# Mamba fronts, tails and column copies divided anew, and the expert bias moved to the front, in a two-layer decoder kernel on one core

## The reference

```python
def mamba(h, inproj, convw, convb, xproj, dtw, dtb, Alog, Dp, outproj):
    xz = jnp.einsum('bld,ed->ble', h, inproj)
    xc, z = jnp.split(xz, 2, axis=-1)
    xc = jax.nn.silu(causal_conv(xc, convw, convb))          # four taps
    xdbl = jnp.einsum('ble,fe->blf', xc, xproj)
    dt = jax.nn.softplus(jnp.einsum('blr,er->ble', xdbl[..., :R], dtw) + dtb)
    ...
    y = ssm_scan(dt, Bm, Cm, xc, A) + xc * Dp    # h = exp(dt A) h + dt x B; y = sum over 16 states of h C
    y = y * jax.nn.silu(z)
    return jnp.einsum('ble,de->bld', y, outproj)
...
for e in range(E):
    gate_e = jnp.sum(jnp.where(top_i == e, top_w, 0.0), axis=-1)
    he = jax.nn.gelu(xf @ w1[e] + b1[e])
    out = out + gate_e[:, None] * (he @ w2[e] + b2[e])
```

## Time and profile before

| | |
|---|---|
| median of 3 runs | 2694.64 us (2692.36 to 2695.38) |
| the profiled execution | 2695.85 us, of which the trace spans 2694.0 us |
| TensorE busy | 2361.3 us (88%) |
| VectorE busy | 1870.9 us (69%) |
| GpSimd busy | 1543.2 us (57%) |
| ScalarE busy | 1339.3 us (50%) |
| layer 0 Mamba | from 3.9 to 1022.5 us, first scan at 66.15 |
| layer 1 Mamba | from 1916.3 to 2451.0 us, first scan at 1973.83 |
| experts | from 1556.1 to 1916.0 us |

### The profile page before, as it was taken

The page is one execution under the profiler, slowest core; times in us unless marked ns, Lnnn a source line. Parts: engine busy times, 40 slices in busy tenths (PEclk is TensorE's granted clock), DMA queues, the critical chain, the costliest instruction groups (busy, mean ns, idle before and its releaser), DMA issues. The chain is left out here.

```text
span 2694.0 us, 28358 instructions
## 1 busy us (share of the span) xinstructions
PE 2361.3 (88%) x8874; PEld 1077.4 (40%) x8874; DVE 1870.9 (69%) x2587; ACT 1339.3 (50%) x2213; POOL 1543.2 (57%) x1356
## 2 busy tenths in 40 slices
PE   7989899898988778888999769999889989688878
PEld 3323333333333223343433349998433333223322
DVE  2999999999999983347777241111379999994334
ACT  4556565655656443444666423332266556453333
POOL 2999999999999971150000112222179999992010
PEclk9999999999999999999999979999789999999989
DMA  4030412303031100043121059996332130300000
GB/s 179 25 125 1 143 52 84 133 10 125 1 125 52 74 0 24 19 123 63 38 39 25 6 188 329 327 329 233 105 126 79 48 125 1 125 1 22 1 9 32
DMA packets 70204, 239.03 MB, mean 89 GB/s; under 512 B 15819, under 2 KB 35799, under 8 KB 47399
## 3 DMA queue, kind: packets, MB, share of 16 engines
q1 hardware_dynamic: 58292, 183.90, 20.3%
q10 hardware_dynamic: 8018, 43.09, 4.6%
q0 software_dynamic: 3744, 10.23, 1.0%
HBM read 220.60 MB, written 16.38 MB: 88 GB/s over the span
## 5 line engine op out<-in xcount | busy, mean ns | idle before, releaser
L896 POOL TENSOR_TENSOR s_dbu<-s_dx,s_bc 128x512 f32<-128x512 f32 x768 | 968.6, 1290 | 26.4 <-DVE s_psum L564 24.8
L480 PE MATMUL s_psum<-s_hc,ident 128*128 128x512 f32 x1536 | 831.1, 634 | 151.9 <-DVE s_hc L584 131.2
L759 ACT ACTIVATE s_psum<-s_dt,s_a_neg 128x512 f32<-128x512 f32 x768 | 521.7, 688 | 576.9 <-DVE s_hc L584 576.0
L480 PEld LDWEIGHTS s_psum<-s_hc,ident 128*128 128x128 f32 x1536 | 263.8, 193 | 657.7 <-DVE s_hc L584 413.8
L584 DVE TENSOR_TENSOR s_hc<-s_psum,s_bc 128x512 f32<-128x512 f32 x624 | 419.8, 673 | 0.4 <-issue 0.4
L564 DVE TENSOR_TENSOR_SCAN s_psum<-s_psum,s_state,s_dbu 128x512 f32<-128x512 f32 x312 | 394.6, 1277 | 11.4 <-POOL s_dbu L896 6.7
L564 DVE TENSOR_TENSOR_SCAN s_psum<-s_psum,s_dbu 128x512 f32<-128x512 f32 x312 | 381.4, 1223 | 14.9 <-POOL s_dbu L896 12.5
L2015 ACT ACTIVATE s_probs<-s_banks 128x512 f32<-128x512 f32 (+3 forms) x384 | 169.6, 495 | 117.1 <-PE s_banks L1724 85.8
L2452 ACT ACTIVATE s_hidden<-s_banks,s_w 128x128 f32<-128x128 f32 x312 | 97.6, 364 | 194.3 <-PE s_banks L2244 192.5
L163 POOL TENSOR_TENSOR s_pair<-s_res 128x512 f32<-128x512 f32 x4 | 5.1, 1280 | 328.5 <-issue 327.1
L907 POOL TENSOR_TENSOR s_hc<-s_hs,s_bc 128x512 f32<-128x512 f32 x144 | 183.6, 1275 | 14.6 <-DVE s_hs L564 14.6
(11 more groups left out here) (325 smaller groups left out, 3272.6 us busy)
## 6 DMA issues: line engine op xcount, KB each, us to landing
s_bc<-fwd_rows SPq DMA_DIRECT2D x64, 1024.0 KB, 4.7
s_w<-in_moe_w SPq DMA_DIRECT2D x39, 1028.0 KB, 5.9
s_w<-in_moe_w ACTq DMA_DIRECT2D x39, 1024.0 KB, 6.8
s_bc<-m_rows SPq DMA_DIRECT2D x32, 1024.0 KB, 4.7
qk_parts<-s_parts SPq DMA_DIRECT2D x48, 128.0 KB, 1.9
s_stack_q<-qk_parts SPq DMA_DIRECT2D x96, 64.0 KB, 2.4
s_stack_k<-qk_parts SPq DMA_DIRECT2D x48, 128.0 KB, 4.4
x<-in_xT SPq DMA_DIRECT2D x4, 512.0 KB, 6.7
```

Of the source, the lines that this page charges most:

```text
L480: pe.matmul(psum[:, SCANS + block_no % 2, :], consts["ident"][:], hc[:, unit % PRODUCTS, :], start=(n == 0), stop=(n == NS - 1)).then_inc( ...
L759: act.activation(psum[:, unit % SCANS, :], dt[:, g % 2, i // NS, :], ACT.Exp, scale=a_neg[CHUNKS[g][0]][:, i:i + 1]).then_inc(decay_ready, 1)
L896: pool.tensor_tensor(dbu[:, unit % TERMS, :], dx[:, g % 2, i // NS, :], bc[:, 2 * n, :], ALU.mult)\
```

## The change

Six edits, all of order or of the engine that does a piece of work. A new small input holds the convolution's taps as columns (`fold`).

1. **Fronts of both Mambas.** The first x chunk and the x half of the weights are loaded first, the taps in two halves. VectorE scales the x half of the weights. The input products of chunk 0 are taken from the centered x and scaled behind the product, by VectorE on its way into `pad`. TensorE convolves blocks 0 and 1; VectorE convolves blocks 2 and 3 (`fold`, 8 instructions). GpSimd adds the two feature halves ahead of mean and variance, so that TensorE needs one product for each of them. dt of blocks 0 and 1 is finished first, dt of blocks 2 and 3 behind unit 2; their two last steps go to GpSimd at units 18 to 24 of chunk 0. The statistics of token chunks 2 and 3 move into chunk 0.
2. **Last columns.** VectorE's 32 `keep` copies of an even chunk become 52 copies on ScalarE, each ahead of the `decay` that overwrites the bank, with a wait in between.
3. **Tails of both Mambas.** The output products of the last chunk begin beside the last units; the last gate product, the scaling and the add to x are VectorE's, from PSUM.
4. **Expert bias.** The bias product (gate x b2) is taken at the experts' front, transposed, and added to x by VectorE in four pieces: two between `low_hot` and `source`, two behind the shares.
5. **Expert blocks.** The first input product is placed ahead of the second block's turn.
6. **Expert tail.** ScalarE multiplies row 0 by its share, VectorE joins in one instruction per tile, TensorE turns into eight banks, four pairs used once.

```diff
+            load_x(0)
             sp.dma_start(w_in[:, :, 0:EI], dram[f"{first}_in"][:, :, 0:EI]).then_inc(in_x_loaded, 16)
-            sp.dma_start(taps[:], dram[f"{first}_taps"]).then_inc(taps_loaded, 16)
+            load_x(1)
             for r, run in enumerate(runs):
                 sp.dma_start(cols[r][:], dram[f"{run[0]}_cols"]).then_inc(small_loaded, 16)
                 sp.dma_start(a_neg[r][:], dram[f"{run[0]}_alog"]).then_inc(small_loaded, 16)
+            sp.dma_start(state[:, 0:TAPS * EB], dram[f"{first}_fold"]).then_inc(small_loaded, 16)
+            sp.dma_start(taps[:, 0:KD * TAPS, :], dram[f"{first}_taps"][:, 0:KD * TAPS, :]).then_inc(taps_first_loaded, 16)
             sp.dma_start(w_x[:], dram[f"{first}_x"]).then_inc(x_loaded, 16)
...
+            def first_in_x(m):
+                if m == 0:
+                    pe.wait_ge(x_scaled, KD)
+                    pe.wait_ge(ln_centered, 1)
...
             mean(0)
+            first_in_x(0)
             mean(1)
...
+                    if g == NC - 1 and i in (58, 59):
+                        last_res(i - 58)
+                    if g == NC - 1 and i in (62, 63):
+                        for m in range(KD):
+                            last_out(m, i - 62)
+            for k in (2, 3):
+                for m in range(KD):
+                    last_out(m, k)
...
-            def keep(g, i):
-
-                unit = g * UNITS + i
-                dve.wait_ge(scanned, unit + 1)
-                at = unit % SCANS
-                if LENT[i - 1]:
-                    dve.tensor_copy(state[:, i:i + 1], psum[:, at, CH - 1:CH]).then_inc(kept, 1)
-                else:
-                    dve.tensor_copy(state[:, i - 1:i + 1].unsqueeze(2), psum[:, at - 1:at + 1, CH - 1:CH]).then_inc(kept, 1)
...
+            def keep_first_x(m):
+                dve.wait_ge(first_x, m + 1)
+                dve.wait_ge(rms_rstd_ready, 1)
+                dve.tensor_tensor(pad[:, m, TAPS - 1:TAPS - 1 + CH], first_bank(m), rms_rstd[0], ALU.mult)\
+                   .then_inc(first_kept, 1)
+            def fold(m, j):
+                tap, total_u = state[:, j * EB + m:j * EB + m + 1], u[:, 0, m, :]
+                if j == 0:
+                    dve.wait_ge(small_loaded, 32 * len(runs) + 16)
+                    dve.wait_ge(front, 1)
+                    dve.wait_ge(first_kept, m + 1)
+                    dve.tensor_scalar(total_u, pad[:, m, 0:CH], tap, None, ALU.mult).then_inc(folded, 1)
+                else:
+                    dve.wait_ge(folded, KD * (j - 1) + m - KD + 1)
+                    dve.scalar_tensor_tensor(out=total_u, in0=pad[:, m, j:j + CH], scalar=tap, in1=total_u,
+                                             op0=ALU.mult, op1=ALU.add).then_inc(folded, 1)
...
+            def last_gate():
+                e, part = EB - 1, dx[:, (NC - 1) % 2, EB - 1, :]
+                dve.wait_ge(gate_ready, NC)
+                dve.wait_ge(y_read, NC * EB)
+                dve.tensor_tensor(part, part, gate[:, e, :], ALU.mult).then_inc(last_gated, 1)
...
+            for k in range(KD):
+                scale_first_in(k)
             center(0)
             center(1)
-            scale_xn(0)
+            for m in range(KD + 1):
+                keep_first_x(m)
+            fold(2, 0)
+            keep_first_x(3)
+            fold(3, 0)
+            for j in range(1, TAPS):
+                for m in (2, 3):
+                    fold(m, j)
+            for c in range(2):
+                scale_xn(c)
...
+                    last = unit - SCANS
+                    act.wait_ge(product_ready, own(last + 1))
+                    if CHUNKS[last // UNITS][2] + 1 < BCH:
+                        act.activation(state[:, last % UNITS:last % UNITS + 1], psum[:, unit % SCANS, CH - 1:CH], ACT.Copy)\
+                           .then_inc(kept, 1)
...
+            first_abs(0)
+            first_abs(1)
+            first_soft(0)
+            for m in (2, 3):
+                first_abs(m)
+                first_relu(m)
+            square_x(2)
...
+                    if g == 0 and i == 2:
+                        first_soft(1)
+                        square_x(3)
...
+                    if g == 0 and i in (18, 22):
+                        add_relu(0, 2 + (i - 18) // 4)
+                    if g == 0 and i in (20, 24):
+                        times_u(0, 2 + (i - 20) // 4)
+                    if g == 0 and i in (35, 40):
+                        scale_res(2 if i == 35 else 3)
...
+            def bias(c):
+                if c == 0:
+                    pe.wait_ge(gate_stored, 1)
+                elif c >= 2:
+                    pe.wait_ge(biased, c - 1)
+                for k in range(KD):
+                    mm = pe.matmul(banks[:, 2 * (c % 2) + k, :], b2[:, k * P:(k + 1) * P], gate_t[:, c * CH:(c + 1) * CH],
+                                   start=True, stop=True)
+                mm.then_inc(bias_ready, 1)
+            bias(0)
+            bias(1)
...
             turn(0)
+            pe.wait_ge(biased, NCH)
+            first(0)
             turn(1)
...
+            add_bias(0)
+            add_bias(1)
...
+            def join(c):
+                for t in range(4 * c, 4 * c + 4):
+                    dve.wait_ge(half_ready, t + 1)
+                    dve.scalar_tensor_tensor(out=rows_in[:, 1, t, :], in0=rows_in[:, 1, t, :], scalar=share[:, 1, t:t + 1],
+                                             in1=rows_in[:, 0, t, :], op0=ALU.mult, op1=ALU.add).then_inc(y_ready, 1)
+            def add_turned(c):
+                dve.wait_ge(y_turned, c + 1)
+                xv = x[:, :, c * CH:(c + 1) * CH]
+                dve.tensor_tensor(xv, xv, banks[:, 2 * c:2 * c + 2, :], ALU.add)
...
+            join(0)
+            for c in range(1, NCH):
+                join(c)
+                add_turned(c - 1)
+            add_turned(NCH - 1)
...
+            act.wait_ge(share_ready, 1)
+            for t in range(NT):
+                if t % 4 == 0:
+                    act.wait_ge(rows_loaded[t // 4], 32)
+                act.activation(rows_in[:, 0, t, :], rows_in[:, 0, t, :], ACT.Copy, scale=share[:, 0, t:t + 1])\
+                   .then_inc(half_ready, 1)
```

362 lines of the change are left out of this document (228 added, 134 removed).

## The result

| | median us (range, runs) | profiled span | granted clock |
|---|---|---|---|
| before | 2695.01 (2692.36 to 2701.36, 4) | 2694.0 | 0.957 |
| changed | 2637.73 (2636.26 to 2639.56, 4) | 2636.0 | 0.959 |

What follows compares the result with a forecast made beforehand. VectorE and GpSimd, both nearly full, bound the chunks; fronts and tails are serial chains. Fronts -40, chunks -3, Mamba tails -15, experts -11 sum to -69 us: forecast 2626 us, own range 2617 to 2635, 8-in-10 range 2608 to 2650.

Steps and rivals of the forecast that it cites:

- The fronts, -35.0 instead of -40: Starts of both Mambas: first scan 21 us earlier in layer 0 and 19 us earlier in layer 1, -40 us.
- the row copy near 34.0: Front of layer 0: the row copy ends near 34.0 us, against 48.0 before, a gain of 14 us.
- two more dt products 41.0: Front of layer 0: the products for dt blocks 2 and 3, behind VectorE's relu at 39.3, end at 41.0 us.
- The spread of B and C: Rival for both fronts: first scan waits for this spread, each front gains only the row copy's 14 us; 2638, 7%.
- The rival with the lower level all through: TensorE stays at its lower clock through the fronts: 18 us per front, 2662, or 2641 up to the convolution; 15%.
- The chunks, +8.2 instead of -3: All chunks together: 3 us shorter, bounded by -20 and +14.
- These chunks get 1 to 2 us longer: Both chunks 0: four more GpSimd instructions, 5 us on 113.58, lengthen each by 1 to 2 us; +3 taken.
- the chunks give it back: Rival: copies ahead of decays and GpSimd's moved work bring the chunks to +14 instead of -3; 2643, 14%.
- an even chunk above 119: Sign in the even chunks: a length above 119 us would make the prediction wrong.
- -10 for the four other even chunks: Even chunks other than the chunks 0: together 10 us shorter, limited by GpSimd's busy time.
- VectorE's saving in full: Rival in the chunks: the saving shows fully down to GpSimd's limit, chunks at -15 to -20; 2612, 12%.
- the decay chain as the limit: Rival in even chunks: product, copy, wait, decay limit every unit, slower than before; 2700, 2%.

Runs made afterwards that it cites:

- the better order: Changed kernel with ScalarE's list in chunks 0 reordered: stores of x behind decays 0 to 3, square behind 4, second half softplus behind 7; 2630.43 us, 0.9758.
- ScalarE's copies alone: Kernel before with one part of the change alone: ScalarE copies the state columns ahead of the decay that overwrites them; 2683.55 us, 0.9955.
- the best version: Changed kernel with ScalarE reorder, all state copies on ScalarE, constant products, later bias addition, dt in the front, res's scaling on GpSimd at terms 18, 24; 2608.25 us, 0.9677.
- steps and res on VectorE: Kernel of the better order with the four dt step operations and the scaling of res's last two quarters on VectorE; 2631.84 us, 0.9758.
- decays first: Kernel of the better order with a chunk 0's first three decays ahead of abs and relu of dt blocks 2 and 3; 2639.67 us, 0.9781.
- copies back: Changed kernel with the copies of the state columns back on VectorE, behind the scan; 2645.15 us, 0.9813.
- GpSimd's copies moved: Changed kernel with GpSimd's twelve state copies of an even chunk moved to ScalarE as well; 2626.92 us, 0.9751.
- steps on VectorE: Kernel of the better order with the four operations making dt and dt*u of blocks 2 and 3 on VectorE instead of GpSimd; 2636.59 us, 0.9776.
- res on VectorE: Kernel of the better order with the scaling of res's last two quarters on VectorE ahead of scans 22 and 26; 2626.60 us, 0.9738.
- dt in the front: Kernel of the better order with dt of blocks 2 and 3 made in the front, as before the change; 2629.49 us, 0.9749.

## Why the prediction was right, and where it was wrong

**The fronts, -35.0 instead of -40.** The chain was the right one: the first scan waits for ScalarE's decay behind dt blocks 2 and 3, through VectorE's `center` 3 and relu. Two terms were mis-sized, 1.8 and 1.0 of the 2.6 us that each chain was longer. One is the rows product: "the row copy near 34.0" was 36.0, since its eight instructions (3.6 us) follow the convolution. The other is "two more dt products 41.0": TensorE had fallen back to its lower clock, and they took 3.78 us instead of 1.7, of which the added 1 us for waits covered a part. The spread of B and C was no limit, so that rival falls.

**TensorE's clock.** The sum had four instructions of the input products at 0.86, and this is what the changed kernel's trace has in both Mambas; the convolution ran at 0.43, the last dt products at 0.86 again. The rival with the lower level all through falls, a piece of it was true. By the Trainium skill, "TensorE: Matmul & The Clock Gate", section "Part 1: The HAM clock gate", the clock falls with idleness and rises after work; the trace agrees (0.50 behind 1.98 us of wait, 1.00 behind the mean and input products), and work of no use in the waits took 2.7 us off the second front. The other rule, from the Trainium skill's page "SBUF — State Buffer", section "Who interferes with whom", would have had the folds wait for GpSimd's instructions at 0.6 us each. One of six did: the first, issued 0.2 us behind GpSimd's scaling of the weights, took 1.17 us, the other five 0.74 each, with GpSimd idle behind the first 0.4 us of them. So the trace agrees with the rule where the two met, and it cost 0.4 us:

```profile
26.36 4.47 DVE L704 SCALAR_TENSOR_TENSOR s_u<-s_pad,s_state,s_u 128x512 f32<-128x512 f32 x6
```

The folds ended at 30.8, not 29, still 1 us ahead of TensorE's convolution.

**The chunks, +8.2 instead of -3: the step that failed.** "These chunks get 1 to 2 us longer" reckoned a chunk 0 as one account, 5 us more on GpSimd's 113.58. Three things were wrong in it. ScalarE's new list was never laid beside TensorE's: it held back the stores of x, so TensorE was late and ScalarE waited for its variances; the better order took 5.1 and 3.5 us off, 3.5 without the clock's part. GpSimd's four operations and res's scaling (ahead of terms 12 and 18 before, 35 and 40 in the changed kernel) fell into the second and third block, where it has no room; with dt of blocks 2 and 3 back in the front the chunks 0 fell by 5.2 and 4.5 us, about half of it in the second block, where GpSimd's four had stood, and most of the rest in the first, which half a softplus had left, and without res's scaling the third block fell by 4.6. In the second Mamba order and dt are 8.0 of the 10.0 us between the changed kernel's chunk 0 (124.81) and that with ScalarE's copies alone (114.82); the best version, with res's scaling moved too, stands at 114.56. And the copies helped the chunks 0 more than I said, 4.2 us each where nothing covers it. The rival "the chunks give it back" had a total of +14 with ScalarE's copies as one of two causes; its size was nearer than mine, the copies were not its cause. By the prediction's own sign, "an even chunk above 119", it was wrong here: both chunks 0 lie above it, and so does chunk 4 with 120.02, which stood at 119.69 before the change already.

"-10 for the four other even chunks" was -4.8, and over the eight kernels with this code -1.8 to -5.9. The reason given, that GpSimd sets the pace, is shown for layer 0 by the run with its copies moved; the size assumed that these chunks come down to GpSimd's busy time, and they stopped 1.4 to 4.1 us above it. Only in the second Mamba, where GpSimd had 3.8 us of room, did VectorE's saving show. A copy on ScalarE took 0.17 us, not 0.35, and slowed no later chunk that the runs show. VectorE's saving in full and the decay chain as the limit both fall.

**Tails and experts, -24.6 instead of -26.** Both as forecast. The experts' tail has the forecast's length partly by another cause, the results' DMA, so that agreement is in part luck; the front's +2.8 was +0.8 to +2.9 over the runs with the same code there.

**What was not foreseen**: 6.6 us in stages that nobody touched, variation of one profiled execution, which by chance fell on the side of the forecast.

## What to carry to other kernels

When two engines feed each other through a ring of a few buffers, cut a stage of the profile into short stretches (here sixteen units of a chunk's 64, the ring holding three terms): an operation costs nothing only if its engine has room in that very stretch, and idle time elsewhere in the stage doesn't pay for it. Before you call a start-up gain, follow what was taken out of the front to the place where it went, and lay the lists of all engines there beside each other. And cut both traces at the same events, so that stages with the same code show how much of a difference is only variation.

## What the hardware showed that was not expected

- In layer 0 the first four instructions of the input products took about 0.86 us each (3.63 in all, at 13.72) in a stretch whose granted clock is given as 1.00; in the second Mamba the same four stand at 0.54. At the start of a program the instructions' pitch tells the clock better than that column.
- With the same code, these four took 3.6 to 3.8 us in four kernels (changed, order, steps and res on VectorE, decays first) and about 2.0 in five (copies back, GpSimd's copies moved, steps on VectorE, res on VectorE, dt in the front). That is 1.7 to 2.0 us up to the row copy of layer 0, and no edit touches it.
- VectorE's `scale_xn`, two inputs on chip, and a term of GpSimd, likewise: in the kernel before the term began 0.12 us earlier and `scale_xn` took 2.23 us (at 72.34); in the changed kernel `scale_xn` began 0.06 us earlier and took 1.21 us (at 77.87), and GpSimd's term took 2.29 instead of 1.27. In both, the one that came first went at its own speed.
- The eight instructions of the experts' last two bias chunks took 7.16 us from 1563.14, about 0.86 each, at a granted clock of 0.50, where the eight of the first two had taken 6.03 us. They set the time of the first expert: with the token indices 1.0 us earlier the stage gained nothing.
- A copy of one 128x1 column on ScalarE, from PSUM, takes 0.17 us (312 in 52.2 us), from SBUF 0.19; the same on GpSimd 0.21.
